# Moving the stacked query and key rows of a two-layer transformer kernel to other partitions

## The chip, the cores and the metric

The kernel runs on one core of one Trainium2 chip. The metric is device time in microseconds (us) of one execution, the median of several. The core has five engines (TensorE, VectorE, ScalarE, GpSimd, SyncE), called PE, DVE, ACT, POOL and SP in the profile, and 16 DMA engines that all queues share.

## The reference

Input x has 16 sequences of 256 tokens with 128 channels. There are two layers. Each is attention with 16 heads of 8 channels, a residual sum and a layer norm, then a mixture of experts, a residual sum and a layer norm. Layer 0 (causal attention; 8 experts, top 2) and layer 1 (full attention with biases; 15 experts, top 3, and a shared expert). What matters here is the score product of each head:

```
q, k, v = split(x @ w_qkv)          # 16 heads of 8 channels
s = einsum('bhqd,bhkd->bhqk', q, k) / sqrt(8)
p = softmax(s)                      # causal in layer 0
o = einsum('bhqk,bhkd->bhqd', p, v)
```

## The kernel before, in words

**A batch.** An attention step `a` is one sequence of one layer; there are 32 (16 per layer). For each the PE computes queries and keys of all heads into one bank (`qk`, L991). ACT copies them to `parts` rounded to the matmul's reduced fp32 type (`qk_hi`, L852) and DVE writes what the rounding left beside it (`qk_lo`, L1225). So `parts` holds, for 128 rows (head and channel), a high and a low part of queries and of keys. A half batch (`u` = 0 or 1) is the eight heads in rows 64u to 64u+63.

**The stacks.** The score product needs high times high, high times low and low times high, summed. The kernel makes these one matmul by stacking along the contraction: `QK` is four tiles of 128 rows, one per half batch in turn (number c % 4 with c = 2a + u), and each row holds eight heads, two sides and 256 tokens (16 KB). `stack` (L676) issues three DMAs on SP's queue, one per product i. Each reads 64 rows of `parts` and writes eight neighbouring rows of the tile, 128 KB in all. For i = 0 and 1 the pieces read are 1 KB long; for i = 2 the two lie side by side and make 2 KB. The tiles are zeroed once at the start in rows 0 to 95 (L758 and L1467), and rows 96 to 127 get zeros for queries and ones for keys. The rows that no stack writes stay zero.

**Who reads them.** `scores` (L1016) multiplies rows 0 to 95 of a tile for the row maximum (DVE, `row_max`), the PE transposes the negated maxima (`max_T`), ACT copies them to `mrow` and issues one DMA of 16 KB on ACT's queue that writes rows 96 and 97 of the same tile (`max_rows`, L883). `scores_T` (L1045) multiplies all 128 rows, now with the maxima in them, and ACT takes the exponential. `scores` waits for the three stack DMAs of its half batch and `scores_T` for the `mrow` DMA. `qk_hi` of the next batch waits until both halves of `parts` have been read, since `parts` is one tile.

**Order.** Every engine runs its steps in an order that `plan` and `lay_out` work out beforehand from costs and due times. It is the same before and after the change. SP's order holds the stacks among the loads of `xT`, `X`, expert weights (`W<-w_in`) and pages, the stores of pages, and the clears of `xs`. After layer 0's attention its experts run beside layer 1's attention.

**Lines.** The change touches L687 and adds a function behind L122. The waits that the prediction speaks of are L684 (stack), L856 (`qk_hi`), L1024 (`scores`, seen in the profile at the matmuls L1027 and L1029) and L1051 (`scores_T`, seen at L1054 and L1056).

Of the kernel before, what the change touches and what calls it, by code (L numbers as in the profile page):

```python
# [5 lines left out]
F32 = mybir.dt.float32  # L6
# [12 lines left out]
HD = D // NH  # L19
# [8 lines left out]
DMA = 16  # L28
# [91 lines left out]

RW1, RX1, RY1 = 7, 8, 4
X_PIECES = ((0, 2), (2, 4), (4, 8), (8, 16))  # L122


BANKS = ("S0", "S1", "T0", "T1", "O", "M", "N", "FH")
# [22 lines left out]
def plan():  # L148
# [4 lines left out]
    def add(due, on, busy, tail, name, *x, after=(), bank=None, frees=None):  # L153
        steps[(name,) + x] = (due, on, busy, tail, after, bank, frees)
# [9 lines left out]
    def attention(a, t):  # L164
# [41 lines left out]
        for blk in range(2):  # L206
# [5 lines left out]
        add(t + 0.3, "ACT", 0.43, 0.1, "O_back_keep", a, after=[("O_back", a)], frees="N")  # L212
        add(t + 0.8, "PE", 0.44, 0.25, "proj", a, after=[("O_back_keep", a), ("residual_bias", a)] + [("load_x", i) for i, (lo, hi) in enumerate(X_PIECES) if lo <= a < hi],
            bank="N")
# [83 lines left out]
    add(-7, "SP", 1.9, 2.8, "load_consts", after=[("load_xT", 0)])  # L298
    for i in range(len(X_PIECES)):
        add(5 + 18 * i, "SP", 0.5, 2.4, "load_x", i, after=[("stack", 2 * i, 1)])  # L300
# [99 lines left out]
def build(nc, x_in, xT_in, cols_in, rows_in, bmat_in, rmat_in, wqk_in, wvo_in, w0_in, w1_in, w2_in, b2_in, sw1_in, out):  # L400
    ctx = ExitStack()
    with ctx:
        def sb(name, shape, dt=F32):
            return ctx.enter_context(nc.sbuf_tensor(name, shape, dt))
# [4 lines left out]
        def signal(name, per=1):  # L409
            return Signal(ctx.enter_context(nc.semaphore(name)), per)  # L410
# [6 lines left out]
        QK = [sb(f"QK{i}", [D, NH // 2, 2, T], F32R) for i in range(4)]  # L417
# [98 lines left out]
        warmed = signal("warmed", 2)  # L516
        x_loaded = [signal(f"x_loaded{i}") for i in range(len(X_PIECES))]
        early_in = signal("early_in")
# [20 lines left out]
        stacked = [signal(f"stacked{i}", 3 * DMA) for i in range(4)]  # L539
# [62 lines left out]
        def wait_x(eng, b):  # L602
            for i, (lo, hi) in enumerate(X_PIECES):
                if lo <= b < hi:
                    eng.wait_ge(x_loaded[i].sem, DMA)
# [25 lines left out]
        def _(sp):  # L631
# [15 lines left out]
            def load_x(i):  # L647
                lo, hi = X_PIECES[i]
                sp.dma_start(X[:, 2 * lo:2 * hi, :], x_in[lo:hi].rearrange("b (c p) d -> p (b c) d", p=D))\
                    .then_inc(x_loaded[i].sem, DMA)  # L650
                if i == 0:
                    sp.dma_start(rows[:, :], rows_in.partition_broadcast(D)).then_inc(rows_loaded.sem, DMA)
# [23 lines left out]
            def stack(a, u):  # L676
                c = 2 * a + u
                sp.wait_ge(lo_done.sem, lo_done.all(a))
                if a < 2:
                    sp.wait_ge(cleared.sem, (2, 4, 7, 10)[c])  # L680
                    if c < 2:
                        sp.wait_ge(cleared_dve.sem, c + 1)
                else:
                    sp.wait_ge(st_ps.sem, st_ps.at(a - 2, 8 * u + 8))  # L684
                p = parts[64 * u:64 * u + 64, :, :, :].bitcast(F32).rearrange("p s i t -> p (s i) t")
                for i, pair in enumerate((p[:, 0::2, :], p[:, 0::3, :], p[:, 1:3, :])):
                    sp.dma_start(QK[c % 4][HD * i:HD * i + HD, :, :, :].bitcast(F32), pair).then_inc(stacked[c % 4].sem, DMA)  # L687

            def table_row(g):
                sp.wait_ge(tabled.sem, tabled.all(g))  # L690
# [37 lines left out]
            def store_out(q):  # L728
# [4 lines left out]

            run_plan({"load_first": load_first, "load_consts": load_consts, "load_xT": load_xT, "load_x": load_x, "load_later": load_later,
                      "clear_xs": clear_xs, "build_w1": build_w1, "stack": stack,
                      "table_row": table_row, "w_load": w_load, "x_load": x_load, "page_store": page_store,
                      "store_out": store_out})
# [808 lines left out]
```

## Time and profile before

| | us |
|---|---|
| median of 3 runs | 1296.94 |
| lowest, highest | 1291.04, 1297.44 |
| the profiled execution's own time | 1286.28 |
| its span | 1284.5 |
| PE busy | 981.0 (76%) |
| DVE busy | 667.5 (52%) |
| ACT busy | 568.1 (44%) |
| POOL busy | 458.6 (36%) |
| mean granted PE clock | 0.857 |

Busy time is time in which an engine had an instruction in work, and "waited" is idle time of the engine before an instruction, put down to what released it. The chain of waits follows the end of the execution back to its start. DMA rates are what the packets of all queues moved in a stretch. A packet's time runs from its start to when the DMA engine is done with it, so data that is still on its way is not in it.

### The profile page before, as it was taken

How to read it: one execution, taken by the hardware profiler on the slowest of the kernel's cores; microseconds unless marked ns; L12 is line 12 of the kernel's file. 1: busy time of each engine (PE TensorE's matmuls, PEld its weight loads, DVE VectorE, ACT ScalarE, POOL GpSimd, SP SyncE). 2: the span in 40 equal slices, each digit the busy share in tenths (PEclk: the TensorE clock that was granted, in tenths of full speed). 3: DMA queues.
4: the chain of work that ended last, by engine and by line, in shares of the span. 5: the costliest groups of instructions: out<-in, count | busy, mean ns of one | idle time of the engine just before them, and what ended most of it. 6: DMA issues, size and time to landing. Idle time of an engine off the chain costs nothing.

```text
span 1284.5 us, 22964 instructions
## 1 busy us (share of the span) xinstructions
PE 981.0 (76%) x7486; PEld 813.4 (63%) x7486; DVE 667.5 (52%) x2161; ACT 568.1 (44%) x1352; POOL 458.6 (36%) x743
## 2 busy tenths in 40 slices
PE   5887978878989866769978866778768999977500
PEld 4776877757878755557766644556556689966400
DVE  4454655455444455646535456557645465556422
ACT  1343544435545424446644543447245544433301
POOL 7000000056000166272000175104873156077675
PEclk9788998889989976989978886889678899989855
DMA  5554466663554322355454222323235269966521
GB/s 84 101 129 80 90 127 141 102 148 77 160 126 109 68 53 51 59 117 115 141 108 88 53 51 45 42 27 61 55 74 113 84 192 317 276 205 187 154 55 43
DMA packets 111510, 138.47 MB, mean 108 GB/s; under 512 B 12036, under 2 KB 85794, under 8 KB 111394
## 3 DMA queue, kind: packets, MB, share of 16 engines
q1 hardware_dynamic: 100002, 114.97, 39.4%
q0 software_dynamic: 10240, 20.99, 6.2%
q10 hardware_dynamic: 1152, 1.05, 0.4%
q8 instruction: 62, 1.02, 0.3%
q14 instruction: 54, 0.44, 0.1%
HBM read 70.25 MB, written 42.48 MB: 88 GB/s over the span
## 4 chain that ended last, share of the span: by engine, by line
PE 48%; DMA 21%; POOL 14%; issue 7%; DVE 4%; ACT 3%; SPq 1%; ACTq 0%; POOLq 0%; DVEq 0%
DMA QK<-mrow 13%; POOL G L837 9%; PE bank_O L1076 7%; PE bank_T L1054 5%; DMA QK<-parts 4%; PE bank_N L1168 4%; PE bank_FH L1156 4%; POOL xs L821 4%; PE bank_S L1031 4%; PE bank_T L1056 3%; PE bank_T L1058 3%; PE bank_S L1027 3%; PE bank_S L1029 3%; PE bank_M L1000 2%; PE bank_N L1084 2%
## 5 line engine op out<-in xcount | busy, mean ns | idle before, releaser
L1242 DVE TENSOR_REDUCE mp<-bank_S 128x3 f32<-128x384 f32 (+1 forms) x512 | 306.5, 619 | 249.0 <-PE bank_S L1031 126.4
L894 ACT ACTIVATE P<-bank_T 128x384 f32<-128x384 f32 (+1 forms) x512 | 263.9, 544 | 213.0 <-PE bank_T L1058 114.6
L837 POOL DMA_INDIRECT G<-yd,ypos x160 | 155.2, 970 | 117.0 <-issue 51.7
L821 POOL DMA_INDIRECT xs<-X,ypos x160 | 155.6, 972 | 54.6 <-issue 49.9
L1054 PE MATMUL bank_T<-QK 128*128 128x256 f32 x512 | 118.6, 342 | 47.7 <-DMA QK<-mrow 42.6
L1027 PE MATMUL bank_S<-QK 96*128 96x256 f32 x512 | 121.7, 340 | 35.6 <-DMA QK<-parts 27.1
L770 POOL TENSOR_TENSOR rstd<-mv,half 128x2 f32<-128x2 f32 x64 | 13.1, 204 | 361.7 <-DVE mv L1295 361.3
L1076 PE MATMUL bank_O<-P,V 128*32 128x256 f32 (+1 forms) x2048 | 134.7, 384 | 9.0 <-ACT P L894 7.3
L1056 PE MATMUL bank_T<-rmat 128*128 128x256 f32 x256 | 96.2, 376 | 45.5 <-DMA QK<-mrow 45.5
L1054 PEld LDWEIGHTS bank_T<-QK 128*128 128x128 f32 x512 | 85.5, 220 | 71.8 <-issue 56.7
L1027 PEld LDWEIGHTS bank_S<-QK 96*128 96x128 f32 x512 | 87.4, 219 | 50.8 <-issue 29.2
L1029 PE MATMUL bank_S<-rmat 128*128 128x256 f32 x256 | 95.1, 371 | 22.4 <-DMA QK<-parts 19.8
L927 ACT ACTIVATE X<-X,rstd 128x128 f32<-128x128 f32 x128 | 55.9, 485 | 123.3 <-POOL rstd L775 123.2
L1031 PE MATMUL bank_S<-QK 96*128 96x128 f32 (+1 forms) x512 | 108.8, 301 | 0.0
L1058 PE MATMUL bank_T<-QK 128*128 128x256 f32 (+1 forms) x512 | 95.7, 272 | 0.0
L1076 PEld LDWEIGHTS bank_O<-P,V 128*32 128x32 f32 x2048 | 58.7, 115 | 54.9 <-issue 29.1
L1058 PEld LDWEIGHTS bank_T<-QK 128*128 128x128 f32 x512 | 90.3, 216 | 0.3
L1056 PEld LDWEIGHTS bank_T<-rmat 128*128 128x128 f32 x256 | 54.9, 214 | 55.6 <-issue 45.6
L1031 PEld LDWEIGHTS bank_S<-QK 96*128 96x128 f32 x512 | 89.5, 213 | 0.3
L901 ACT ACTIVATE OT<-bank_O 128x256 f32<-128x256 f32 x128 | 49.1, 384 | 90.3 <-PE bank_O L1076 88.1
L1447 DVE SCALAR_TENSOR_TENSOR X<-G,wk,X 128x128 f32<-128x128 f32 x160 | 46.2, 355 | 76.7 <-DMA G<-yd,ypos 76.7
L1029 PEld LDWEIGHTS bank_S<-rmat 128*128 128x128 f32 x256 | 54.2, 212 | 30.6 <-issue 22.8
(167 smaller groups left out, 1752.9 us busy)
## 6 DMA issues: line engine op xcount, KB each, us to landing
QK<-parts SPq DMA_DIRECT2D x192, 128.0 KB
QK<-wtab SPq DMA_DIRECT2D x76, 257.0 KB, 3.8
W<-w_in SPq DMA_DIRECT2D x46, 321.0 KB, 3.5
QK<-xs SPq DMA_DIRECT2D x38, 256.0 KB, 4.4
yd<-P SPq DMA_DIRECT2D x38, 256.0 KB, 3.3
xs<-zeros SPq DMA_DIRECT2D x17, 512.0 KB, 8.0
xp<-xs SPq DMA_DIRECT2D x22, 256.0 KB, 3.6
yd<-yb SPq DMA_DIRECT2D x22, 256.0 KB, 2.3
```

The costliest lines, as they stand in the source:

```text
L821: pool.indirect_dma_start(xs[g % 2], bass.IndirectOffsetOnAxis(ypos[L][:, 2 * b + blk, k:k + 1], 0), X[:, 2 * b + blk, :], None).then_inc( ...
L837: pool.indirect_dma_start(G[i][:, blk, k, :], None, yd[g], bass.IndirectOffsetOnAxis(ypos[L][:, 2 * b + blk, k:k + 1], 0))\
L894: act.activation(P[:, (h // 4) % 2, h % 4, 0:n], bank[("T0", "T1")[h % 2]][:, 0:n], ACT.Exp, scale=SCALE)\
L927: act.activation(z, z, ACT.Identity, bias=rstd[:, k, q, 3, blk:blk + 1], scale=rstd[:, k, q, 1, blk:blk + 1]).then_inc(normed[k].sem, 1)
L1027: m = pe.matmul(S[:, qb * T:(qb + 1) * T], Q[:, qb * D:(qb + 1) * D], K)
L1029: pe.matmul(diagonal(S), identr, mask_q, start=True, stop=False, skip_group_check=True)
L1031: m = pe.matmul(S[:, o:o + n], Q[:, qb * D:(qb + 1) * D], K[:, 0:n], start=False, stop=(qb == 1), skip_group_check=True)
L1054: m = pe.matmul(S[:, kb * T:(kb + 1) * T], K[:, kb * D:(kb + 1) * D], Q)
L1056: pe.matmul(diagonal(S), identr, mask_k, start=True, stop=False, skip_group_check=True)
L1058: m = pe.matmul(S[:, o:o + n], K[:, kb * D:(kb + 1) * D], Q[:, kb * D:T], start=False, stop=(kb == 1), skip_group_check=True)
L1076: m = pe.matmul(o, w, x, start=(kb == 0), stop=(kb == 1), skip_group_check=True)
L1242: dve.tensor_reduce(mp[:, a % 2, 0:n, h], bank[("S0", "S1")[h % 2]][:, 0:n * w] .rearrange("p (a c) -> p a c", a=n), AX.X, ALU.max).then_i ...
```

## The change

Product i of half batch c goes to rows 32 i + 8 (c % 4) up to eight rows further. Before, it went to rows 8 i to 8 i + 7 for every c. So tile 0 now uses rows 0-7, 32-39 and 64-71; tile 1 rows 8-15, 40-47 and 72-79; tile 2 rows 16-23, 48-55 and 80-87; tile 3 rows 24-31, 56-63 and 88-95. The sizes, the number, the queue and the order of the DMAs, and all matmuls, stay as they were.

```diff
+def stack_rows(c, i):
+
+    lo = 32 * i + HD * (c % 4)
+    return slice(lo, lo + HD)
...
                 for i, pair in enumerate((p[:, 0::2, :], p[:, 0::3, :], p[:, 1:3, :])):
-                    sp.dma_start(QK[c % 4][HD * i:HD * i + HD, :, :, :].bitcast(F32), pair).then_inc(stacked[c % 4].sem, DMA)
+                    sp.dma_start(QK[c % 4][stack_rows(c, i), :, :, :].bitcast(F32), pair).then_inc(stacked[c % 4].sem, DMA)
```

## Rows read from the trace of the kernel before

**Rows 1.** The page: the chain that ended last, by engine and by line.
```profile
PE 48%; DMA 21%; POOL 14%; issue 7%; DVE 4%; ACT 3%; SPq 1%; ACTq 0%; POOLq 0%; DVEq 0%
DMA QK<-mrow 13%; POOL G L837 9%; PE bank_O L1076 7%; PE bank_T L1054 5%; DMA QK<-parts 4%; PE bank_N L1168 4%; PE bank_FH L1156 4%; POOL xs L821 4%; PE bank_S L1031 4%; PE bank_T L1056 3%; PE bank_T L1058 3%; PE bank_S L1027 3%; PE bank_S L1029 3%; PE bank_M L1000 2%; PE bank_N L1084 2%
```

**Rows 2.** Waits: who waited for whom, us in total, times, longest.
```profile
PE bank_T L1056 <- DMA QK<-mrow: 45.5, 13, 5.9
PE bank_T L1054 <- DMA QK<-mrow: 42.6, 14, 7.8
ACT parts L858 <- DMA QK<-parts: 29.9, 3, 12.0
PE bank_S L1027 <- DMA QK<-parts: 27.1, 8, 5.6
PE bank_S L1029 <- DMA QK<-parts: 19.8, 4, 6.2
```

**Rows 3.** The chain in order of time: start, us, what.
```profile
13.54 11.66 DMA QK<-parts
...
31.53 10.66 DMA QK<-mrow
...
64.47 4.52 DMA QK<-mrow
...
647.92 10.92 DMA QK<-mrow
...
932.92 5.33 DMA QK<-mrow
...
965.14 7.46 DMA QK<-parts
...
1001.27 2.25 DMA QK<-mrow
```

**Rows 4.** Timeline, first two batches: start, us, instruction, idle before and releaser.
```profile
9.97 4.19 SPq L687 DMA_DIRECT2D QK<-parts  x6
...
19.12 0.55 PE L1029 MATMUL bank_S<-rmat 128*128 128x256 f32 x1 [6.20 <-DMA QK<-parts]
...
25.31 0.60 ACT L858 ACTIVATE parts<-bank_M 128x512 fp32r<-128x512 f32 x1 [11.96 <-DMA QK<-parts]
```

**Rows 5.** DMA of 684 to 690 us: busy tenths, GB/s in 40 slices.
```profile
DMA  0354445676545565635855675642827245737999
GB/s 0 96 96 82 75 123 191 164 82 55 48 41 48 48 55 48 61 55 109 109 55 48 55 62 48 61 41 27 82 27 82 27 82 109 96 41 75 113 99 99
```

**Rows 6.** DMA issues, page first, then 684 to 690: count, KB each, us to landing.
```profile
W<-w_in SPq DMA_DIRECT2D x46, 321.0 KB, 3.5
...
W<-w_in SPq DMA_DIRECT2D x1, 321.0 KB, 10.5
```

**Rows 7.** Stretches: us, busy by engine (PE, PEld, DVE, ACT, POOL), clock, DMA share, GB/s.
```profile
658.00:659.00 1.00, 0.02 (x1) 0.05 (x1) 0.00 (x0) 0.00 (x0) 0.00 (x0) 0.50 0.53 205
```

**Rows 8.** Timeline around 648 us, columns as in rows 4.
```profile
643.05 4.11 SPq L687 DMA_DIRECT2D QK<-parts  x6
...
647.92 0.62 ACTq L886 DMA_DIRECT2D QK<-mrow  x1
...
658.98 0.77 PE L1054 MATMUL bank_T<-QK 128*128 128x256 f32 x2 [3.10 <-DMA QK<-mrow]
```

## The prediction

> **What bounds the kernel now.** I read the page's chain first. It gives 48% to PE and 21% to DMA, and 13% of it is the `mrow` DMA and 4% the stacks from `parts` [rows 1]. The chain in order of time puts numbers to these: 13.2% and 4.3% of 1284.5 us are 225 us. 23 pieces of the `mrow` DMA and 7 of the `parts` DMA, each some 4 to 12 us long, carry nearly all of it; the first and last of either kind and one of the longest stand in [rows 3]. The table of waits says that PE stood still in 27 of these places for `mrow` (88 us) and in 12 for `parts` (47 us), and ACT in 3 more [rows 2].
>
> An `mrow` DMA moves 16 KB and takes 2.25 us from issue to landing when nothing is before it, the last in [rows 3]. The others are slow because they come behind stacks: at 643.05 SP issues six stack DMAs, ACT issues its `mrow` DMA at 647.92, and PE gets going on it at 658.98 [rows 8]. So the price of an `mrow` on the path is the rest of the stacks' transfer. What decides about the change is how long a stack takes.
>
> The rate of a stack is in the GB/s row of 684 to 690 us, where stacks run alone until about the last half microsecond and a slice is 0.15 us [rows 5]. It shows a fill (75 to 191 GB/s, slices 2 to 9), then a flat stretch at 41 to 61, mean 51 (slices 10 to 18), a peak of 109 twice (19 and 20), a flat one at mean 53 (slices 21 to 27), 2 KB packets that alternate 27 and 82 (mean 54), and a peak again at slices 34 and 35. Peak to peak are 15 slices, 2.25 us, which is one DMA of 128 KB. Other work shows that the DMA engines can do more: 205 GB/s moved once the stacks were gone [rows 7]. And the stacks hold up what is queued with them: an expert's weights land in 3.5 us, but in 10.5 us there [rows 6]. So a stack DMA is bound by something tied to its eight destination rows (I take it so; that it is the source isn't excluded), and at each change to another group of rows there is a short time in which the old rows still take data and the new ones already do. That is how I read the peaks.
>
> **The change, part by part.** Nothing is added or removed: 192 stack DMAs of 128 KB, 64 `mrow` DMAs, the same matmuls over 96 and 128 rows, the same waits and order. `stack_rows` is worked out when the program is built. PE, DVE, ACT and POOL: 0, since the forms stay and a zero row costs what a full one does. SP's issues: 0, since the pattern has the same dimensions. What is left is the transfer.
>
> *Within one DMA*: eight neighbouring rows before, eight after, at the same kind of boundary. 0.
>
> *From one DMA to the next.* At the flat rate of 52 GB/s, the mean of the two flat stretches, 128 KB (131,072 B) take 2.52 us. Measured are 2.25 us between peaks [rows 5]. The first two half batches give less: PE is released by the first half's three DMAs at 19.12 and ACT by the second half's at 25.31, 6.19 us for three, 2.06 each [rows 4]. So an overlap at a change of rows is worth 0.27 us by the one and 0.46 by the other; I take 0.35. Before, all three changes in a half (0-7, 8-15, 16-23, and back to 0-7) lead to other rows close by, and each has its peak. After, the steps are 32 rows within a half and about 56 back to the next half. No row of the trace shows a step of 32 or 64. From below: all three overlaps stay, 0. From above: the two steps within a half lose it and the odd rows don't help, 2 x 0.46 = 0.92 us per half. I take that one of them is lost, the step of 32 and not that of 64: 0.35 us per half, or 5% of its 6.5 us. It lies near the middle of the bounds, and nothing in the rows excludes that a step which always keeps the same place within a group of 32 rows shares more with its predecessor than the steps of eight did. The Trainium skill, "SBUF — State Buffer", section "Door 1: The DMA port swizzle", says that a partition and the one 32 above it are on the same DMA port, that a step of 64 changes the port, and that each port takes about 27 GB/s. By that rule eight aligned rows are two ports, an estimate of 54 GB/s from its figure, where the flat rate here is 52: the trace agrees there. By it the old layout changed ports at every step and the new one doesn't between products 0 and 1, so it speaks against this change.
>
> *The `mrow` DMA* writes rows 96 and 97 as before. Product 2 now writes rows 64 to 95, which may or may not share a path with them. It starts when the stacks before it are through, so I put nothing.
>
> *On the path.* 30 pieces of the chain wait for stacks (23 and 7). Each waits for at least one half: 30 x 0.35 = 10.5 us. Where an `mrow` waits from behind both halves, as in [rows 8], it is 0.7, so the upper end with this price is 21 us. I stay at 10.5, since the mean piece (225 / 30 = 7.5 us) is little more than one half's 6.5. The other half batches' delays lie under PE's work on the batch before (the chain doesn't go through them). If that cover is gone, 64 x 0.35 = 22 us.
>
> *The clock.* At the end of a long wait the granted clock is 0.50 [rows 7], 1.2 instead of 2.4 GHz, after PE stood nearly idle. Longer waits can put a few more matmuls at the lower level. I have no price for a wait that grows by 0.35 us and put nothing; it can only add.
>
> **Sum.** Made against the profiled execution: 1286.28 + 10.5 = 1296.8 us. That execution lay 10.7 us below the median of the runs, so on the median it is 1296.94 + 10.5 = 1307.4, rounded 1307 us (+0.8%).
>
> **The rivals.**
> *No effect.* A step of 32 rows keeps its overlap (what limits is finer than the pair of row groups 32 apart), or the limit is at the source, which the change doesn't touch. For it: the trace can't tell destination from source. Against it: the source rows don't change between the three DMAs of a half, yet each has its peak. Time: 1297 us.
>
> *More is lost.* Both steps within a half lose the overlap, or product 2 gets in the way of loads that write the upper rows, such as the weights, which already take 10.5 us behind stacks [rows 6]. 0.7 us per half, over 30 pieces 21 us: 1318 us.
>
> *Faster.* The place is product 2, the price its overlap. If rows from 64 up hang on a side of their own, then its 128 KB can drain while product 1 before it and product 0 of the next half drain on the lower side. The overlap at these two steps would be longer than now: the fill shows that the DMA engines hand over up to 191 GB/s for a short time [rows 5]. If these two overlaps go from 0.35 to 0.9 us each and that between products 0 and 1 is lost, a half gains 2 x 0.55 - 0.35 = 0.75 us, and 30 pieces 22 us: 1275 us. It decides from the point where the two overlaps exceed 0.53 us each. Against it: a DMA engine takes its descriptors in turn, the flat stretches show that it holds back once a buffer is full, and that buffer doesn't grow by another destination. A mild form, to 0.65 each, gives 30 x 0.25 = 7.5 us, 1289 us, and is the likelier of the two.
>
> *It doesn't do what it says.* All three products could still stand on the same path; then it falls together with "more is lost", the slower end.
>
> **How the numbers follow.** Forecast (one overlap lost) 0.40, more lost 0.13, no effect 0.30, faster 0.17. The forecast lies 10 us above the median with the runs' own spread of 6 us and the price's lower end (30 x 0.27 = 8) about it, so a good part of it can end within 0.5%. A measurement can't tell less than 0.5%, 6.5 us, from no change. Of the forecast 0.33 is slower and 0.07 the same; of no effect 0.25 is the same, 0.03 slower and 0.02 faster; "more" is all slower; of faster 0.14 is faster and 0.03 the same. That gives slower 0.49, same 0.35, faster 0.16. The range goes from 1287, which holds the mild form of faster, to 1319, which holds "more is lost".
>
> **What would show it.** In the profile after, the GB/s row of a stretch with stacks alone has its peak between products 0 and 1 gone (a flat stretch of about 5 us at 50 GB/s, then a peak) and the peaks around product 2 still there. The landings of the first two half batches lie 6.5 us apart instead of 6.19. The chain's share for `mrow` and `parts` goes from 225 to about 235 us, and PE's waits for them from 135 to some 145. Product 0 to 1 with its peak as before means no effect. Flat stretches above 60 GB/s mean that I was wrong on what limits a stack. A time below 1290 makes the prediction wrong; so does a slower one whose waits for `mrow` and `parts` haven't grown.

## The result, and the profile after

The changed kernel takes 1320.93 us (median of 4 runs, 1319.7 to 1330.7), the one before 1294.01 us (median of 4, 1291.04 to 1297.44). The ratio is 1.0238, 95% interval 1.02 to 1.0277. So it is slower by some 27 us by the medians (their quotient is 1.0208) and 31 us by the ratio, whose interval holds both. I had forecast slower, but 10 us, and a range that ended at 1319. The profiled executions lie 7.7 us (before) and 1.2 us (after) below these medians, so a difference of two traces holds some 6 us of spread between executions.

All of it arises while attention runs. Two views show that. The chain in order of time has its first and its last `mrow` piece at 33.29 and 1034.92 us, against 31.53 and 1001.27 before [rows 3]: the shift grows from 1.8 to 33.7 us, and the span grew by 33.4.

```profile
13.54 13.24 DMA QK<-parts
33.29 10.99 DMA QK<-mrow
...
1034.92 2.24 DMA QK<-mrow
```

The page and the waits after, in the places of [rows 1] and [rows 2]. The chain holds DMA at 24% where it held 21%. Of that, `mrow` and `parts` are 14.3 and 4.0% of 1317.9 us, 241 us where it was 225 (I had forecast 235); the rest of the rise is other DMAs that the chain now goes through.

```profile
PE 46%; DMA 24%; POOL 14%; issue 7%; DVE 4%; ACT 3%; SPq 1%; ACTq 0%; POOLq 0%; DVEq 0%
```

```profile
PE bank_T L1062 <- DMA QK<-mrow: 55.7, 14, 6.7
PE bank_T L1060 <- DMA QK<-mrow: 49.1, 14, 7.9
...
PE bank_S L1033 <- DMA QK<-parts: 30.2, 8, 6.1
PE bank_S L1035 <- DMA QK<-parts: 23.9, 4, 7.3
```

The number of waits is that of before (28 and 12 in place of 27 and 12), but they are longer: 158.9 us against 135.0. PE's busy time went from 981.0 to 989.5 us with the same 7486 matmuls. The mean granted clock fell from 0.857 to 0.852, which is worth some 6 us of it (981.0 x 0.857 / 0.852 = 986.8). 23.9 and 8.5 us make up 32.4 of the 33.4 us by which the two traces differ.

The rate of the stacks, in the stretch that answers to [rows 5] (it begins 1.12 us after SP issues the same six DMAs, 0.15 us a slice):

```profile
DMA  0345445667472656665556445682828272455999
GB/s 0 89 82 96 82 102 177 184 75 75 41 61 27 55 55 55 55 55 55 48 55 61 41 41 48 61 75 21 82 27 82 27 82 27 82 96 82 154 144 79
```

The flat level is as before, 41 to 61 GB/s (one slice has 27). The peak that stood at slices 19 and 20 is gone: from slice 11 to 26 the row has no rise, through the whole change from product 0 (rows 0-7) to product 1 (rows 32-39). The next rise, where product 1 gives way to product 2 (rows 64 and up), comes at slices 36 to 38 where it was at 34 and 35. The landings of the first two half batches, in the place of [rows 4], went from 19.12 and 25.31 us to:

```profile
20.18 0.55 PE L1035 MATMUL bank_S<-rmat 128*128 128x256 f32 x1 [7.25 <-DMA QK<-parts]
...
26.89 0.60 ACT L864 ACTIVATE parts<-bank_M 128x512 fp32r<-128x512 f32 x1 [13.54 <-DMA QK<-parts]
```

### The profile page after: what moved, and what is told of

Read it like the earlier page. It is cut to its first block, busy times and chain, and to the rows that moved or that the text cites. A ratio compares the mean times of both kernels' runs of the same rounds, so it can differ in the third digit from the quotient of the medians.

```text
span 1317.9 us, 22964 instructions
## 1 busy us (share of the span) xinstructions
PE 989.5 (75%) x7486; PEld 821.6 (62%) x7486; DVE 667.0 (51%) x2161; ACT 568.2 (43%) x1352; POOL 457.5 (35%) x743
## 3 DMA queue, kind: packets, MB, share of 16 engines
q8 instruction: 62, 1.02, 0.3%
## 4 chain that ended last, share of the span: by engine, by line
PE 46%; DMA 24%; POOL 14%; issue 7%; DVE 4%; ACT 3%; SPq 1%; ACTq 0%; POOLq 0%; DVEq 0%
DMA QK<-mrow 14%; POOL G L843 9%; PE bank_O L1082 6%; PE bank_T L1060 5%; DMA QK<-parts 4%; PE bank_FH L1162 4%; PE bank_N L1174 4%; POOL xs L827 4%; PE bank_S L1033 3%; PE bank_T L1062 3%; PE bank_T L1064 3%; PE bank_S L1037 3%; DMA G<-yd,ypos 3%; PE bank_S L1035 2%; PE bank_M L1006 2%
## 5 line engine op out<-in xcount | busy, mean ns | idle before, releaser
L1060 PEld LDWEIGHTS bank_T<-QK 128*128 128x128 f32 x512 | 87.8, 226 | 79.0 <-issue 64.2
L1033 PEld LDWEIGHTS bank_S<-QK 96*128 96x128 f32 x512 | 89.6, 224 | 52.1 <-issue 32.0
L1035 PE MATMUL bank_S<-rmat 128*128 128x256 f32 x256 | 95.6, 373 | 26.1 <-DMA QK<-parts 23.9
L1064 PEld LDWEIGHTS bank_T<-QK 128*128 128x128 f32 x512 | 92.2, 220 | 0.3
L1037 PEld LDWEIGHTS bank_S<-QK 96*128 96x128 f32 x512 | 90.2, 215 | 0.3
```

The source lines that it names most:

```text
L1033: m = pe.matmul(S[:, qb * T:(qb + 1) * T], Q[:, qb * D:(qb + 1) * D], K)
L1035: pe.matmul(diagonal(S), identr, mask_q, start=True, stop=False, skip_group_check=True)
L1037: m = pe.matmul(S[:, o:o + n], Q[:, qb * D:(qb + 1) * D], K[:, 0:n], start=False, stop=(qb == 1), skip_group_check=True)
L1060: m = pe.matmul(S[:, kb * T:(kb + 1) * T], K[:, kb * D:(kb + 1) * D], Q)
L1064: m = pe.matmul(S[:, o:o + n], K[:, kb * D:(kb + 1) * D], Q[:, kb * D:T], start=False, stop=(kb == 1), skip_group_check=True)
```

## The experiments

Each of these kernels is the changed one with other rows (or another order) for the three products. Each ratio is to the kernel before on the same chip. "First pair" is the second of the two landings just shown, 25.31 us before and 26.89 after; in the last four runs ACT no longer waits there.

| kernel | rows of products 0, 1, 2 | ratio, 95% interval | first pair lands |
|---|---|---|---|
| changed | 0, 32, 64, plus 8 per tile | 1.0238 (1.0200 to 1.0277) | 26.89 |
| step of 32 | 0, 32, 64 | 1.0297 (1.0249 to 1.0346) | 26.61 |
| own rows | 0, 8, 16, plus 24 per tile | 1.0046 (1.0016 to 1.0076) | 25.23 |
| other order | as changed, issued 0, 2, 1 | 1.0057 (1.0025 to 1.0089) | 25.58 |
| dose | 8, 0, 32 and 0, 32, 8 | 1.0286 (1.0251 to 1.0321) | 26.41 |
| step of 32, low | 0, 32, 8 | 1.0182 (1.0154 to 1.0211) | 26.14 |
| upper | 0, 8, 64 | 1.0103 (1.0077 to 1.0129) | 25.57 |
| upper, 72 | 0, 8, 72 | 1.0051 (1.0021 to 1.0080) | 25.54 |
| every 2nd row | 0, 2, ... / 1, 3, ... / 16, 18, ... | 0.9097 (0.9058 to 0.9137) | no wait for it |
| every 8th | i, i + 8, ..., i + 56 | 0.9198 (0.9173 to 0.9224) | no wait for it |
| every 4th | i, i + 4, ..., i + 28 | 0.8984 (0.8931 to 0.9037) | no wait for it |
| every 12th | i, i + 12, ..., i + 84 | 0.9019 (0.8979 to 0.9060) | no wait for it |

### The two halves of the change, and the order

**Step of 32 alone** (the tiles share rows again):

```diff
-    lo = 32 * i + HD * (c % 4)
+    lo = 32 * i
```

> Products 0, 1 and 2 of every half batch go to rows 0-7, 32-39 and 64-71, so the step of 32 rows stays and the rows of its own for each of the four tiles are undone. Theory A (two DMAs one after the other whose rows lie 32 apart share their path, so the overlap between them is lost, 33 us over 64 half batches): as slow as the changed kernel, 1318 to 1325 us, with the peak of the GB/s row between products 0 and 1 missing. Rival B (it is the rows of its own): back to 1294 us. Rival C (product 2 in rows 64 and up is in the way of loads that write there): 1321 us as well, so this run does not part A from C.

Measured 1330.02 us, 1.0297, 5 us above what I gave and a little slower than the changed kernel (1.0297 and 1.0238, the intervals overlap). Theory A and rival C both survive, and rival B (the rows of its own) falls. The peak between products 0 and 1 (slices 19 and 20) is missing:

```profile
GB/s 0 89 89 96 75 102 205 164 82 62 48 41 48 48 55 48 61 48 55 48 48 55 41 41 61 48 82 34 68 41 55 55 41 41 55 82 143 195 38 123
```

**Own rows alone:**

```diff
-    lo = 32 * i + HD * (c % 4)
+    lo = 3 * HD * (c % 4) + HD * i
```

> Each of the four tiles keeps rows of its own, but the three products follow each other 8 rows apart (rows 24 t + 8 i for tile t). Theory A: every step leads to another path, so the time is that before the change, 1291 to 1298 us, and every product has its peak. Rival B: 1321 us. Rival C: tiles 2 and 3 write rows 64 to 95 in 4 of 12 DMAs, as many as in the changed kernel, so 1315 to 1321 us.

Measured 1295.47 us, 1.0046. It is 0.5% and not nothing, but a fifth of the changed kernel's loss. This kernel writes rows from 64 up in 4 of 12 DMAs, as the changed one does, and with no step of 32; what such rows cost comes below.

**Another order.** The data ends up in the very same rows; only the issue order differs:

```diff
-                for i, pair in enumerate((p[:, 0::2, :], p[:, 0::3, :], p[:, 1:3, :])):
+                for i, pair in ((0, p[:, 0::2, :]), (2, p[:, 1:3, :]), (1, p[:, 0::3, :])):
```

> The rows are exactly those of the changed kernel; only the order in which SP issues a half's DMAs is other: products 0, 2, 1. So no two DMAs in a row are 32 rows apart. Theory A: back to 1291 to 1300 us, with a peak at every product. Rivals B and C, and any reason in where the data lies: 1321 us.

Measured 1301.98 us, 1.0057 (a little over what I expected, by the median). Three quarters of the loss go with no row moved, so it isn't where the data lies but what follows what. The GB/s row of the same stretch has its peak back (slices 18 to 20), and the 2 KB packets of product 2 (the slices that alternate) now come ahead of it:

```profile
GB/s 0 82 89 96 96 102 191 184 68 89 27 68 27 68 27 82 41 96 109 96 34 61 27 62 55 48 55 61 55 48 61 89 109 75 48 41 55 157 106 140
```

### How much one lost overlap costs, and what the upper rows cost

**Dose:**

```diff
-    lo = 32 * i + HD * (c % 4)
+    lo = ((HD, 0, 32), (0, 32, HD))[c % 2][i]
```

> The lost overlap is doubled. Even half batches write products 0, 1, 2 to rows 8-15, 0-7, 32-39, odd ones to rows 0-7, 32-39, 8-15, so of the six steps of a batch four lead to rows 32 away or to the same rows (0 to 32, 32 to 0, 0 to 32, and 8 to 8 of the next batch), against two in the run with rows 0, 32 and 64. All rows are below 64. Theory A (each such step has its price, whatever the tile): twice the 27 to 38 us, 1346 to 1368 us. Rival C (upper rows cost, steps don't): 1292 us, since no upper row is written.

A miss: 1325.94 us, 1.0286, where 1346 to 1368 us was expected. I had made two mistakes. I had counted four lost steps in six, with the last product of a batch and the first of the next as one of them. But a batch's first stack follows no other: `qk_hi` waits until the last batch's stacks have landed (25.31 us in [rows 4]), and only then are the next ones issued (26.66). So a batch has five steps at most (four where its halves are issued too far apart to meet), and here at most three of them are lost (0 to 32, 32 to 0, 0 to 32), against two in the kernels with one step of 32 per half. And I had taken all of the loss for lost steps. With up to three lost steps and no upper row the loss is that of the run with rows 0, 32 and 64, so two can't be the whole of that run's. The next two runs part it.

**Step of 32, no upper rows** (two lost steps a batch):

```diff
-    lo = 32 * i + HD * (c % 4)
+    lo = (0, 32, HD)[i]
```

> Products 0, 1 and 2 of every half batch go to rows 0-7, 32-39 and 8-15. One step in three is 32 rows, and no upper row is written. Theory A with C as a second part: the run with four lost steps in six and no upper rows took 1.029, this one has two in six, so 1.014 to 1.019 (18 to 25 us), and together with the run of the upper rows it makes up the changed kernel's 1.024. If A is all and a second lost step in a row costs nothing more: 1.024 to 1.029. If the upper rows were the main cost: below 1.005.

Measured 1316.5 us, 1.0182: inside what was expected. The peak between products 0 and 1 is missing as in the changed kernel (slices 19 and 20), and the first pair lands 0.83 us later than before:

```profile
GB/s 0 96 96 75 89 102 198 164 82 62 48 48 41 48 55 55 55 55 55 48 61 48 48 41 48 41 96 21 82 27 82 27 82 27 82 96 109 161 79 75
```

```profile
19.53 0.55 PE L1035 MATMUL bank_S<-rmat 128*128 128x256 f32 x1 [6.61 <-DMA QK<-parts]
...
26.14 0.60 ACT L864 ACTIVATE parts<-bank_M 128x512 fp32r<-128x512 f32 x1 [12.80 <-DMA QK<-parts]
```

```profile
1027.77 2.25 DMA QK<-mrow
```

The last line is from its chain in order of time. The first pair gives the price: the first half lands 0.41 us later than before (19.12), both together 0.83, so 0.42 per lost step. The dose, with three in this batch, has its first pair 1.10 us later, 0.37 per step, and its loss is 1.6 times this one's. In the whole, the ratio gives 0.0182 x 1293 = 23.5 us (20 to 27 by the interval), and the last `mrow` DMA is issued 26.5 us later than before (1001.27 [rows 3]). A difference of two traces is rough: in the run with own rows, whose first pair lands no later than before, the last `mrow` is issued at 1006.37, 5.1 us later.

Where does it arise? The issues of the stacks of the second, third and fourth batch, before and then in this run:

```profile
26.66 4.04 SPq L687 DMA_DIRECT2D QK<-parts  x6
...
50.11 2.04 SPq L687 DMA_DIRECT2D QK<-parts  x3
...
71.96 1.98 SPq L687 DMA_DIRECT2D QK<-parts  x3
```

```profile
27.49 4.04 SPq L693 DMA_DIRECT2D QK<-parts  x6
...
51.69 2.04 SPq L693 DMA_DIRECT2D QK<-parts  x3
...
74.27 1.97 SPq L693 DMA_DIRECT2D QK<-parts  x3
```

They come 0.83, 1.58 and 2.31 us later, some 0.77 a batch: these batches pay for both of their halves. Not all batches do. The `mrow` DMAs of the eleventh batch's first half and the fourteenth's second half, before and then in this run:

```profile
295.44 0.62 ACTq L886 DMA_DIRECT2D QK<-mrow  x1
...
406.93 0.62 ACTq L886 DMA_DIRECT2D QK<-mrow  x1
```

```profile
307.72 0.62 ACTq L892 DMA_DIRECT2D QK<-mrow  x1
...
419.72 0.62 ACTq L892 DMA_DIRECT2D QK<-mrow  x1
```

The first comes 12.28 us later, the last 12.79: three batches and more add 0.5 us, where 0.83 each would be 2.5. The chain before runs through POOL and PE there (from 298.97 us on) and waits for stacks in one place, at 372.57. So the delay adds up where the chain waits for stacks, and is covered elsewhere. It isn't an even price either: the first eleven batches add up 12.28 us, 1.1 a batch, and what they pay beyond 0.83 isn't explained.

**Upper rows, no step of 32:**

```diff
-    lo = 32 * i + HD * (c % 4)
+    lo = (0, HD, 64)[i]
```

> Products 0, 1 and 2 of every half batch go to rows 0-7, 8-15 and 64-71. No step is 32 rows, so only the upper rows can cost (theory C as a second part beside A: product 2 is then written to the side where other transfers, which are not held up behind the stacks, write their upper rows). The run with products in the order 0, 2, 1 left 0.6% over the kernel before, so: 1.004 to 1.010 of it, 5 to 13 us. If the upper rows cost nothing: ratio 1.000. If they are the main cost: 1.02.

Measured 1304.22 us, 1.0103, at the upper end. In the stretch with stacks alone the peak stands (116 and 102 at slices 19 and 20), though in the first batch the first half lands at 19.58, 0.46 us later than before, and the pair 0.26 later:

```profile
GB/s 0 89 82 96 82 102 191 171 75 75 41 61 27 55 55 55 55 55 116 102 55 61 48 62 61 55 55 27 82 0 82 27 109 109 109 14 75 21 178 72
```

Most of what the upper rows cost comes late: the `mrow` DMA that was issued at 406.93 is issued at 409.35 here, the last one at 1013.73 in place of 1001.27. That suggests, and doesn't show, that they cost where other transfers are under way. 0.0182 and 0.0103 make 0.0285; the run with rows 0, 32 and 64 for all tiles has 0.0297 and the changed kernel 0.0238.

**Product 2 in rows 72-79:**

```diff
-    lo = 32 * i + HD * (c % 4)
+    lo = (0, HD, 72)[i]
```

> As the run with rows 0-7, 8-15 and 64-71 (1.0103 of the kernel before), but product 2 goes to rows 72-79. What of the upper rows costs? If it is that rows 64-67 share a path with rows 96 and 97, to which the mrow DMA writes and for which PE waits: that sharing is gone, 1.000 to 1.004. If it is that the upper side is the one on which the other transfers write: nothing changes, 1.008 to 1.012.

Measured 1297.73 us, 1.0051, between the two expectations. It suggests that some of the cost of rows 64-71 is the meeting with the `mrow` DMA's rows 96 and 97, but the intervals (1.0021 to 1.0080, and 1.0077 to 1.0129) touch, and what remains isn't explained. In the changed kernel only one tile in four writes rows 64-71. If that tile pays 0.0103 and the other three 0.0051, the mean is 0.0064, near the 0.0057 and 0.0046 of the runs with another order and with own rows; with 0.0182 it makes 0.0246, where the changed kernel has 0.0238. This is an estimate from the runs. Of the upper rows' 7 to 13 us (by the two ratios) the cause stays open.

### What bounds a stack DMA

**Every 4th row:**

```diff
-    lo = 32 * i + HD * (c % 4)
-    return slice(lo, lo + HD)
+    return slice(i, i + 4 * HD - 3, 4)
```

> Product i goes to the eight rows i, i + 4, ..., i + 28 in place of eight neighbouring rows; nothing else changes. Theory A in its full form (a DMA is bound by the few paths that its eight neighbouring rows share): the DMA touches eight paths, 128 KB take about 1.3 us in place of 2.2, a half 3.8 us in place of 6.5, and of the 225 us of the chain some 90 go: 1180 to 1230 us. Rival (the flat rate of 52 GB/s is set by the source rows or by the eight DMA engines): 1290 to 1297 us.

Measured 1163.83 us (1155.51 to 1166.34), 0.8984: 10% faster than the kernel before, and below the range that I gave. The sources, the eight partitions' count, the sizes and the queue are unchanged. The rate in the same stretch, then from the timeline the landing of the first half (19.12 before) and the issue of six stack DMAs:

```profile
GB/s 0 82 82 96 102 102 177 184 191 178 164 171 157 157 164 164 150 82 55 109 177 157 171 191 184 191 184 198 184 198 198 218 191 150 96 21 175 168 103 154
```

```profile
15.12 0.55 PE L1034 MATMUL bank_S<-rmat 128*128 128x256 f32 x1 [2.20 <-DMA QK<-parts]
...
603.55 4.08 SPq L692 DMA_DIRECT2D QK<-parts  x6
```

Its waits, and the issue of weights in that stretch (columns as in [rows 6]):

```profile
PE bank_T L1061 <- DMA QK<-mrow: 10.3, 8, 3.1
PE bank_T L1059 <- DMA QK<-mrow: 10.2, 9, 3.9
```

```profile
W<-w_in SPq DMA_DIRECT2D x1, 321.0 KB, 3.6
```

The rate stays at 150 to 198 GB/s for the most part (168 in the mean of slices 7 to 34, with a dip to 55 at slice 19), where it fell to 50 before. The source is out as a limit. PE's waits for `mrow` fall from 88 to 20.5 us, and the weights behind the stacks land in 3.6 us in place of 10.5 [rows 6]. Six stack DMAs are now issued in 4.08 us, 0.68 each, and 131,072 B in 0.68 us are 193 GB/s: SP's issue is now near the pace of the transfer (that it sets it is not tested). On the chain DMA holds 8% and POOL 24%:

```profile
PE 49%; POOL 24%; issue 10%; DMA 8%; DVE 4%; ACT 3%; SPq 1%; ACTq 0%; POOLq 0%; DVEq 0%
```

**Every 2nd, every 8th, every 12th.** They ask how far rows have to lie apart.

```diff
# every 2nd
+    lo = (0, 1, 2 * HD)[i]
+    return slice(lo, lo + 2 * HD - 1, 2)
# every 8th
+    return slice(i, i + 8 * HD - 7, 8)
# every 12th
+    return slice(i, i + 12 * HD - 11, 12)
```

> Product 0 goes to rows 0, 2, ..., 14, product 1 to rows 1, 3, ..., 15, product 2 to rows 16, 18, ..., 30: eight rows over a span of 16. Theory A, with a path for each four neighbouring rows: a DMA touches four paths instead of two, its flat rate is about 104 GB/s, a half takes some 3.9 us, and the time is 1180 to 1215 us. Rival (any spread will do, for instance since two DMA engines then never write neighbouring rows): 1155 to 1170 us as with every fourth row. Rival (only a row to itself in each group of four helps): 1290 us.

> Product i goes to rows i, i + 8, ..., i + 56. Theory A with rows 32 apart on one path: the eight rows are four paths of two rows each (0 with 32, 8 with 40, 16 with 48, 24 with 56), so the time is that of the run with every second row, within 10 us, and not that with every fourth row, though the rows lie farther apart. Rival (groups 32 apart are paths of their own): eight paths, 1155 to 1170 us.

> Product i goes to rows i, i + 12, ..., i + 84: eight groups of four rows, six of them below row 64 and two above, none 32 apart. Theory A: eight paths, 1155 to 1170 us as with every fourth row, perhaps a few us less since the load is spread over both sides. Rival C (rows of 64 and up get in the way of loads): 10 us or more above the run with every fourth row.

Measured 1170.38 (0.9097), 1185.37 (0.9198) and 1162.44 us (0.9019). The rows of the same stretch, in this order:

```profile
GB/s 0 89 89 89 75 109 177 198 178 198 164 137 109 109 109 123 109 123 150 184 102 96 102 109 116 150 171 109 109 102 116 109 109 109 109 116 123 144 195 208
```

```profile
GB/s 0 102 102 89 75 123 198 191 191 184 143 109 109 116 116 75 96 109 109 109 109 102 82 82 102 89 89 102 96 96 82 96 103 89 89 102 161 161 130 154
```

```profile
GB/s 0 96 102 75 89 109 191 191 191 191 164 191 157 184 157 150 164 157 171 171 171 150 164 157 171 171 123 164 143 157 164 212 178 137 89 41 144 144 137 188
```

Every second row has a flat level of 109, twice that of neighbouring rows. Its peaks (184, then 171, at slices 20 and 27) are those where product 2 takes over and where it gives way; between products 0 and 1, which lie in the same rows 0 to 15, there is none. Every eighth row, though spread four times as wide, is no better: 109 down to 82 (75 once). Every twelfth row goes nearly like every fourth, 123 to 191 for the most part. So four neighbouring rows are one path, and rows 32 apart are the same path: with every 8th row, eight rows fall on four paths.

The rule of the Trainium skill, "SBUF — State Buffer", section "Door 1: The DMA port swizzle", is that a DMA port serves four neighbouring partitions and the four 32 above them, and that a step of 64 goes to another. By it neighbouring, 2nd, 8th, 4th and 12th rows reach 2, 4, 4, 8 and 8 ports; the trace agrees with 52, 109, 82 to 109, and 168 in the mean for both of the last.

Two misses of size. Every 2nd row ran in 1170.38 us, below the 1180 that I had expected and at the edge of the rival's 1155 to 1170, so the time alone doesn't decide; the flat level of 109 against 168 does. And every 8th row lies 15 us above it, where I had given 10. There all three products stand on the same four paths, so no step has an overlap, and its row has no peak before slice 37; with every 2nd row only the step from product 0 to 1 is such a one. That is a likely reason, not a tested one, and that the rate goes down to 82 to 103 isn't explained by it. Rival C would have every 12th row 10 us or more above every 4th, and fails: 0.9019 and 0.8984 have intervals that overlap, with two rows in eight above row 64.

## Why the prediction was wrong

**What bounds the kernel: right.** The stacks in front of `mrow` do; made faster they give back 10%. That it is the destination rows and not the source was an assumption, and every 4th row shows it.

**Within one DMA, 0: right.** The flat level of the changed kernel is 41 to 61 GB/s as in [rows 5]. PE, DVE and ACT have their instruction counts and, but for the clock, their times.

**From one DMA to the next: right in the place, about right in the price.** I took it that the overlap is lost at the step of 32 and kept at that of 64. The peak went at just that step, and issuing the products in another order brought it back. Taken were 0.35 us per half; the run that has nothing but this step shows 0.42. My "all three changes in a half" was one too many: after a batch's last stack comes no other until it has landed, so a batch of six has five changes at most.

**The upper rows, "I put nothing": wrong.** Alone they cost 1.0103, and 1.0051 with eight rows' shift, 7 to 13 us; in the changed kernel some 0.0056 (1.0238 less 1.0182), 7 us. I had this as a part of the rival "more is lost". Its cause stays open.

**On the path, 30 x 0.35: the step that failed.** I let each of the 30 pieces pay for one half batch, because the mean piece (7.5 us) is little more than one half's 6.5. The run with the step alone loses 23.5 us (20 to 27), 0.78 us per piece, and that is about what both halves lose, 0.83. The reason can be read in [rows 8]: SP issues the two halves' six DMAs back to back, and the `mrow` DMA gets through behind all six. In the kernel before ten of the 32 batches are issued so; in 14 others the halves come less than 8 us apart, when the first can still be in transfer (it needs 9.15 us from issue to landing in [rows 4]). That both halves are on the path there too is read off the delay, not followed wait by wait. The chain names only the part of the transfer after `mrow` was issued, since before that it goes through PE. But the end of the transfer, which is what PE waits for, moves by the whole of what six DMAs grew, however short the piece is. The first batches show it one by one, with 0.83, 0.75 and 0.73 us (the third has its halves issued apart). The case was in the prediction as the upper end, 30 x 0.7 = 21 us; with 0.42 per half it is 25.

The other half of that step, "the other half batches' delays lie under PE's work", holds at least where the chain doesn't wait for stacks: from 295 to 407 us the delay grew by 0.5 us. "If that cover is gone, 64 x 0.35" therefore isn't what happened, though 64 x 0.42 = 27 us comes to nearly the same. The sum can't tell 30 pairs from 64 halves; the stretch does. How the delay is spread over the other batches (1.1 us each in the first eleven) stays open.

**The clock, "nothing, it can only add": it added** some 6 of the 8.5 us by which PE's busy time differs between the two traces, as part of these waits' cost and not beside them: the ratio of the step alone holds it too. How much of the 6 us is spread between executions isn't known.

So with the place of the loss right, the time came out by the rival "more is lost" (1318 us, chance 0.13), for another reason than it gave: not a second lost overlap, but one lost overlap paid for by both halves (23.5 us), and some 7 us for upper rows, 31 us together by the ratios. Of the signs named ahead, the missing peak and the longer waits came, the waits by 24 us and not by 10; "landings 6.5 us apart" came as 6.71, and the first of them late by 1.06 us, which I hadn't foreseen: 0.41 is the step's (the run with the step alone), and 0.46 the upper rows' (the run with these alone).

## What to carry to other kernels

When a wait ends with a transfer, count how much the whole queue of transfers ahead of it grows, from where they were issued; the chain shows only the last piece. Where the chain runs through other work, the growth is covered. A DMA that writes few partitions should spread them: here every 4th row in place of eight in a row triples the rate of the stacks and makes the kernel 10% faster with one line changed. And among DMAs that follow each other on a queue, rows 32 apart are no change of place.

## What the runs showed of the hardware

- The rate of a DMA that writes eight partitions depends on which: 41 to 61 GB/s for neighbours, 109 for every 2nd, 75 to 116 for every 8th, 168 in the mean for every 4th and every 12th.
- When one DMA follows another to rows on other paths, the two overlap for a short time, worth 0.42 us at 128 KB per DMA here. Rows 32 higher give no overlap. Two lost overlaps a batch cost 1.0182, two to three cost 1.0286.
- In the one stretch looked at, a small DMA on ACT's queue didn't pass those on SP's. From 648.6 to 657.4 us of the kernel before no packet of ACT's queue (q10) moved, though its `mrow` DMA was issued at 647.92 [rows 8]; all 18 (16 of data) came in the 1.2 us after. SP's queue (q1) moved 1.12 MB meanwhile, more than the 0.79 MB of the six stacks. The Trainium skill, "DMA: Bandwidth & Descriptors", section "Queues, rings and completion order", has each DMA engine take turns between queues; the trace doesn't show turns here.

The view of DMA queues of the kernel before (packets, MB, share of the engines), 648.6 to 657.4 first and then 657.4 to 658.6:

```profile
q1 hardware_dynamic: 859, 1.12, 94.0%
...
q1 hardware_dynamic: 138, 0.22, 49.4%
q10 hardware_dynamic: 18, 0.02, 3.9%
```
